# A cross-attention and mixture-of-experts layer: value projections of the second batch moved into the opening, first maxima split by key halves

## Chip, cores and metric

One core of a Trainium2 chip runs the whole layer in one launch. The metric is device time in microseconds (us), from the first to the last instruction of the program with what the launch adds around it; lower is better.

## The reference

Four batches of 512 tokens of width 256. First cross-attention over 1024 context tokens with 16 heads of width 16, rotary positions and a mask; then a second layer with causal self-attention and a mixture of 8 experts, of which each token takes 2.

```python
# x (4,512,256), ctx (4,1024,256), mask (4,1024)
query = split_heads(layernorm(x) @ w_q.T); key = split_heads(ctx @ w_k.T); value = split_heads(ctx @ w_v.T)
query, key = rope(query), rope(key)
scores = einsum('bhqd,bhkd->bhqk', query, key) / sqrt(16)
scores = where(mask == 0, -10000.0, scores)
x = x + (softmax(scores) @ value) @ w_o.T
h = layernorm(x)
h = h + causal_attention(layernorm(h, ln1)) @ proj.T
gate = softmax(layernorm(h, ln2) @ router.T); two best experts of 8
x = x + h + sum_e weight_e * gelu(ln2(h) @ w1_e) @ w2_e
```

The kernel holds every matmul input as a high and a low part, so a projection is three products (high with high, high with low, low with high) over two halves of the width: 6 matmuls of 128x512, or 6 of 128x256 for half a job.

## The kernel before

The change lies in `cross_attention`, the first of three blocks. `attention_order` writes one list of jobs by hand; each engine walks that list and does its own share of every job, in order, waiting on counters of the other engines (`by_pe`, `by_dve`, `by_act`, `by_pool`). The jobs:

- `w`: split of a weight. ACT makes the high part (L575), then DVE or POOL the low part (L467). `wv` and `wo` are POOL's.
- `c(b,g)`: split of half g (512 tokens) of batch b's context, brought by SP into the one buffer `craw`; for b > 0 on POOL (L498, L467).
- `xn`, `xT`, `q`: layer norm, transposition, query projection of a batch.
- `k(b,g,e)` and `v(b,g,n)`: key and value projections of a context half (PE L824). ACT copies each product out (L612) into `turn_a` or `vaug`, except in the first batch's queries and `k(0,0,*)`, which DVE takes.
- `rope(b,part)`: the rotation and its split (function `turn`, L450 to L464), on DVE for `(0,2)` (queries) and `(0,0)`, else on POOL. SP stores its parts to DRAM (`store_turned`), then loads them back in the layout of the scores (`load_queries`, `load_keys`) into `qst` and `kst`, one unit of 8 heads at a time.
- `max(quad,hp,qt,kh)`: 2 score matmuls into one of two `wide` slots (PE L910) and a reduction (DVE L756) that gives row maxima of a quad (4 heads); 16 of these, then `nm` (DVE L760 to L766), `mxt` (PE L915, ACT) and `load_max_rows` on SP bring the maxima into `qst`.
- `rate(1)`: DVE's statistics of batches 1 to 3 (L675 to L686), with a square root on ACT (L566) between.

After the list `before` (the opening) come 128 groups, 32 to a batch. A group is 4 score matmuls (PE L949), 4 exponentials (ACT L618) and 8 weighing matmuls of the group before (PE L964). Between them stand 2 maxima of the next quad, and at most a job or so of projection work for the next batch, placed by the due times in `timed`. Values of batch 1 are projected in half jobs in groups 13 to 20. Projections, scores and `mxt` share three `narrow` PSUM slots in a ring: the job that takes a slot waits until what stood in it three places earlier has been copied out. From group 118 on there are no maxima left and two scores are taken together.

In the opening the order is: `k(0,1,*)`, queries, `k(0,0,*)`, then `wv` and `wo`, the four `v(0,..)`, `rate(1)`, `c(1,0)`, `k(1,0,*)`, `rope(1,0)`, `c(1,1)`, 16 maxima of quad 0, then 4 maxima of quad 1 with the two jobs `k(1,1,*)` among them. POOL's own order follows from it: `rope(0,1)`, `wv`, `wo`, `c(1,0)`, `rope(1,0)`, `c(1,1)`, `rope(1,1)`.

## Time and profile before

| what | value |
|---|---|
| median of 3 runs | 791.83 us (788.49 to 794.24) |
| the profiled execution | 785.16 us, of which the span of instructions is 783.4 us |
| mean granted TensorE clock | 0.948 |

```profile
span 783.4 us, 13504 instructions
## 1 busy us (share of the span) xinstructions
PE 694.3 (89%) x4402; PEld 424.7 (54%) x4402; DVE 557.6 (71%) x919; ACT 493.5 (63%) x980; POOL 354.6 (45%) x262
## 2 busy tenths in 40 slices
PE   2355799999999999999999999879978879999996
PEld 1252344444444443444333433557767768889985
...
ACT  1110567788777788777777778566645057667673
POOL 4867435129440359068658920000055703544444
PEclk9775789999999999999999999999989899999999
DMA  9476257665868473338858820089437456533321
GB/s 264 164 249 184 113 178 245 208 165 192 272 205 238 121 231 114 116 147 282 282 202 291 272 112 2 1 294 421 108 84 251 156 119 139 96 36 36 39 28 20
DMA packets 59719, 130.73 MB, mean 167 GB/s; under 512 B 8868, under 2 KB 26308, under 8 KB 58196
```

Section 1 is busy time; section 2 cuts the span into 40 slices of 19.6 us with a digit of busy tenths each. The opening is the first four to five slices, the groups of the cross-attention run to about the twenty-fifth, and the second layer fills the rest.

### The profile page before, as it was taken

What the parts mean: (1) busy time and instruction counts of PE and PEld (TensorE: products, weight loads), DVE (VectorE), ACT (ScalarE), POOL (GpSimd) and SP (SyncE); (2) the same over time, 40 slices, a digit from 0 to 9 for tenths busy, and PEclk for the clock granted to TensorE, in tenths of its full rate; (3) what the DMA queues carried; (4) which work ended last, traced back from release to release, by engine and by line L of the source; (5) the groups of instructions that cost most, each with busy time, mean ns of one, the idle gap of its engine ahead of it and who ended that gap; (6) DMA issues with size and microseconds to landing.
All of it is one profiled execution on the core that took longest, in us unless ns stands there. A gap on an engine that the chain in (4) does not pass through costs nothing. (4 is left out here: it accounts for less than half of the span.)

```text
span 783.4 us, 13504 instructions
## 1 busy us (share of the span) xinstructions
PE 694.3 (89%) x4402; PEld 424.7 (54%) x4402; DVE 557.6 (71%) x919; ACT 493.5 (63%) x980; POOL 354.6 (45%) x262
## 2 busy tenths in 40 slices
PE   2355799999999999999999999879978879999996
PEld 1252344444444443444333433557767768889985
DVE  4968778778888778887889893367985435555553
ACT  1110567788777788777777778566645057667673
POOL 4867435129440359068658920000055703544444
PEclk9775789999999999999999999999989899999999
DMA  9476257665868473338858820089437456533321
GB/s 264 164 249 184 113 178 245 208 165 192 272 205 238 121 231 114 116 147 282 282 202 291 272 112 2 1 294 421 108 84 251 156 119 139 96 36 36 39 28 20
DMA packets 59719, 130.73 MB, mean 167 GB/s; under 512 B 8868, under 2 KB 26308, under 8 KB 58196
## 3 DMA queue, kind: packets, MB, share of 16 engines
q1 hardware_dynamic: 33364, 72.86, 28.2%
q0 software_dynamic: 16848, 35.95, 17.9%
q10 hardware_dynamic: 9440, 21.06, 9.0%
q8 instruction: 38, 0.62, 0.3%
q14 instruction: 29, 0.24, 0.1%
HBM read 80.80 MB, written 69.39 MB: 192 GB/s over the span
## 5 line engine op out<-in xcount | busy, mean ns | idle before, releaser
L756 DVE TENSOR_REDUCE mx<-wide 128x2 f32<-128x1024 f32 x256 | 307.3, 1222 | 69.3 <-PE wide L910 68.1
L618 ACT ACTIVATE probs<-narrow 128x512 f32<-128x512 f32 x492 | 265.4, 599 | 73.5 <-PE narrow L949 72.3
L910 PE MATMUL wide<-kst,qst 49*128 49x512 f32 x512 | 177.2, 475 | 14.7 <-DMA kst<-k_pieces 7.8
L949 PE MATMUL narrow<-qst,kst 51*128 51x512 f32 x492 | 186.2, 451 | 2.5 <-ACT probs L618 2.2
L949 PEld LDWEIGHTS narrow<-qst,kst 51*128 51x128 f32 x492 | 79.0, 185 | 133.8 <-issue 49.6
L964 PE MATMUL values<-probs,vaug 128*17 128x512 f32 x1024 | 135.3, 600 | 1.4 <-ACT probs L618 0.8
L1714 POOL DMA_INDIRECT out<-res,token x39 | 60.7, 1557 | 94.4 <-DMA out<-res,token 60.5
L910 PEld LDWEIGHTS wide<-kst,qst 49*128 49x128 f32 x512 | 71.4, 194 | 29.4 <-DVE mx L756 16.9
L1246 POOL DMA_DIRECT2D out<-xt x4 | 5.5, 1378 | 113.8 <-DVE xt L1441 113.8
L1739 ACT ACTIVATE h_hi<-narrow 128x512 fp32r<-128x512 f32 x39 | 23.3, 599 | 42.5 <-PE narrow L1819 42.5
L455 POOL TENSOR_TENSOR turn_b<-turn_a,tab 128x1024 f32<-128x1024 f32 x10 | 24.0, 2401 | 55.6 <-ACT turn_a L612 55.1
L1765 DVE TENSOR_TENSOR h_lo<-narrow,h_hi 128x512 fp32r<-128x512 f32 x39 | 27.0, 692 | 23.8 <-ACT h_hi L1739 23.8
L964 PEld LDWEIGHTS values<-probs,vaug 128*17 128x17 f32 x1024 | 17.0, 95 | 44.4 <-issue 29.5
L1253 POOL DMA_INDIRECT list_rows<-lists,rows_to x32 | 32.2, 1008 | 17.2 <-issue 8.5
L1761 DVE TENSOR_TENSOR y_lo<-y_full,y_hi 128x256 fp32r<-128x256 f32 x39 | 16.6, 425 | 30.0 <-ACT y_hi L1726 30.0
L450 POOL TENSOR_SCALAR keep<-keep 128x512 f32<-128x512 int32 x7 | 13.6, 1942 | 51.8 <-ACT turn_a L612 51.8
L1725 ACT ACTIVATE y_full<-wide,lncol 128x128 f32<-128x128 f32 x78 | 35.8, 459 | 0.9 <-PE wide L1796 0.9
L1726 ACT ACTIVATE y_hi<-wide,lncol 128x128 fp32r<-128x128 f32 x78 | 36.3, 465 | 0.0
L498 POOL CAST c_hi<-craw 128x1024 fp32r<-128x1024 f32 x6 | 6.2, 1038 | 59.8 <-PE narrow L824 57.9
L824 PE MATMUL narrow<-wv_hi,c_hi 128*128 128x256 f32 x64 | 16.3, 340 | 15.0 <-POOL wv_lo L467 15.0
L612 ACT ACTIVATE vaug<-narrow 128x256 f32<-128x256 f32 (+1 forms) x28 | 11.6, 416 | 28.3 <-PE narrow L824 27.0
L1810 PE MATMUL wide<-w_hi,y_hi 128*128 x78 | 28.6, 448 | 0.0
(289 smaller groups left out, 1350.3 us busy)
## 6 DMA issues: line engine op xcount, KB each, us to landing
list_rows<-in_w ACTq DMA_DIRECT2D x56, 342.0 KB, 5.4
kst<-k_pieces SPq DMA_DIRECT2D x14, 784.0 KB
k_pieces<-turn_a SPq DMA_DIRECT2D x16, 512.0 KB, 4.3
w_hi<-w_hi SPq DMA_DIRECT2D x16, 512.0 KB, 11.0
w_lo<-w_lo SPq DMA_DIRECT2D x16, 512.0 KB, 11.9
turn_a<-in_w POOLq DMA_DIRECT2D x11, 512.0 KB, 5.3
w_hi<-turn_b POOLq DMA_DIRECT2D x11, 512.0 KB, 3.0
w_lo<-turn_a POOLq DMA_DIRECT2D x11, 512.0 KB, 4.5
```

Source lines behind the costliest of these rows:

```text
L455: step(engine.tensor_tensor(z[:, :, :], a[:, :, :], cos, ALU.mult))
L618: nc.scalar.activation(probs[:, n % NP, :], score_bank(n), ACT.Exp, scale=DK ** -0.5).then_inc(exp_done, 1)
L756: last = nc.vector.tensor_reduce(mx[quad % 2][:, qt, :, hp, kh], slot[:, :, :], axis=AX.X, op=ALU.max)
L910: last = nc.tensor.matmul(slot[:, i, :], qst[u % 3][r:r + R_MAX, h, P * qt:P * qt + P], kst[u % 3][r:r + R_MAX, h, 512 * kh:512 * kh + 512 ...
L949: nc.tensor.matmul(score_bank(n), kst[u % 3][r:r + R_ALL, h, P * kt:P * kt + P], qst[u % 3][r:r + R_ALL, h, :], start=True, stop=True).the ...
L964: last = nc.tensor.matmul(values[32 * hq:32 * hq + DK + 1, :], vaug[b % 2][:, kt, h, :], probs[:, (4 * g + hq) % NP, :], start=kt == 0, st ...
L1253: pool.indirect_dma_start(list_dram, bass.IndirectOffsetOnAxis(rows_to[:, j, i, s:s + 1], 0), lists[j][:, i, s, :].bitcast(U32), None).the ...
L1714: pool.indirect_dma_start(out, bass.IndirectOffsetOnAxis(token[:, n:n + 1], 0), res[n % PIECES][:, :], None, bounds_check=TOKENS - 1, oob_ ...
L1725: nc.scalar.activation(yT[n % 2][:, k, :], y_banks[n % 2][:, k, :], ACT.Identity, **affine)
L1726: last = nc.scalar.activation(yT_hi[n % 2][:, k, :], y_banks[n % 2][:, k, :], ACT.Identity, **affine)
L1765: nc.vector.tensor_tensor(hT_lo[n % 2][:, :, :], h_banks[n % 2], hT_hi[n % 2][:, :, :].bitcast(F32), ALU.subtract).then_inc(h_lo_set, 1)
L1810: last = nc.tensor.matmul(up_banks[n % 2], a[n % 2][:, k, :], w[:, bass.ds(e, 1), k, :].rearrange("p e n -> p (e n)"), start=(i, k) == (0, ...
```

## The change

- `w v` moves ahead of `rope(0,1)` on POOL; `w o` moves behind `c(1,1)`, and on ACT behind `rate(1)`.
- `k(0,0,*)` leaves the ring and is written to the `wide` slots.
- `c(1,1)` gets a landing place of its own (`next_raw`, which is `xn`), loaded early; it moves ahead of `rope(1,0)`.
- A job `heat`: 18 matmuls of the identity that nobody reads, once `rope(0,1)` is done.
- The values of batch 1 (`v(1,..)`, four whole jobs) are projected in the opening, between `k(1,0,*)` and the maxima, and no longer in groups 13 to 20.
- The 16 maxima of quad 0 go by key half: 8 with `kh` = 1, which need only the second half of the keys, then 8 with `kh` = 0. The loads get counters of their own (`quad_in`, `half_in`), and SP loads the first two heads' keys before the other queries.
- `k(1,1,*)` is cut into four half jobs, two straight behind the last maximum and two behind the first two maxima of quad 1. The loads of unit 1 (`load_queries(1)`, `load_keys(1)`) move behind `load_max_rows(0)`.
- The due times of the loop come from a table `PLAN`: group offsets for `xn`/`xT`, `q`, `v`, `c`, `k` and `oP` per batch. Batch 2's queries are now made in batch 0's groups (26 to 30), its keys in groups 9 to 19 (before: 21 to 28); `load_context(2,1)` on SP stands behind the store of batch 1's queries.

The diff without declarations and the lines that only thread the new names through:

```diff
@@ -35,6 +35,10 @@
 
 AHEAD = 4
 LEAD = 3
+PLAN = [(18, (26, 27, 28, 30), (), (3, 12), (9, 10, 11, 14, 16, 17, 18, 19), ()),
+        (None, (), (4, 5, 6, 7, 9, 10, 11, 12), (7, 16), (18, 19, 20, 22, 23, 24, 25, 27), (13, 14, 15, 16)),
+        (-6, (3, 4, 6, 7), (13, 14, 15, 16, 17, 18, 19, 20), (), (), (8, 10, 11, 12)),
+        (None, (), (), (), (), (8, 10, 11, 12))]
 
 
 def final(order, *begin):
@@ -48,24 +52,31 @@
     def maxes(quad):
         return [("max", quad, hp, qt, kh) for hp in range(2) for qt in range(QT) for kh in range(2)] + [("nm", quad), ("mxt", quad)]
 
-    before = [("rate", 0), ("xn", 0), ("w", "q"), ("c", 0, 1), ("w", "k"), ("mask", 0), ("xT", 0), ("k", 0, 1, 0), ("k", 0, 1, 1), ("rope", 0, 1), ("c", 0, 0),
-              ("q", 0, 0), ("q", 0, 1), ("rope", 0, 2), ("k", 0, 0, 0), ("k", 0, 0, 1), ("rope", 0, 0), ("w", "v"), ("w", "o")]
+    before = [("rate", 0), ("xn", 0), ("w", "q"), ("c", 0, 1), ("w", "k"), ("mask", 0), ("xT", 0), ("k", 0, 1, 0), ("w", "v"), ("k", 0, 1, 1), ("rope", 0, 1), ("c", 0, 0),
+              ("q", 0, 0), ("q", 0, 1), ("rope", 0, 2), ("k", 0, 0, 0), ("k", 0, 0, 1), ("rope", 0, 0)]
     before += [("v", 0, g, n) for g in range(2) for n in range(2)]
-    before += [("rate", 1), ("c", 1, 0), ("k", 1, 0, 0), ("k", 1, 0, 1), ("rope", 1, 0), ("c", 1, 1)] + maxes(0)
-    before += [*maxes(1)[:2], ("k", 1, 1, 0), *maxes(1)[2:AHEAD], ("k", 1, 1, 1), ("rope", 1, 1)]
+    before += [("rate", 1), ("c", 1, 0), ("c", 1, 1), ("w", "o"), ("heat", 0), ("k", 1, 0, 0), ("k", 1, 0, 1), ("rope", 1, 0)] + [("v", 1, g, n) for g in range(2) for n in range(2)]
+    before += [("max", 0, hp, qt, kh) for kh in (1, 0) for hp in range(2) for qt in range(QT)] + [("nm", 0)]
+    last = [("k", 1, 1, n // 2, n % 2) for n in range(4)]
+    before += last[:2] + [("mxt", 0)] + maxes(1)[:2] + last[2:] + maxes(1)[2:AHEAD] + [("rope", 1, 1)]
 
     timed = []
     for b in range(B):
         g, t = 32 * b, b + 1
-        if t < B:
-            timed += [(max(g - 6, 0) + n * (1 if b else 0.3), ("xn", t, n)) for n in range(QT)] + [(g + (0.5 if b else 2.5), ("xT", t))]
-            timed += [(g + x, ("q", t, n // 2, n % 2)) for n, x in enumerate((3, 4, 6, 7) if b else (4, 5, 6, 7))] + [(g + 7.5, ("rope", t, 2))]
-            timed += [(g + 13.2 + n, ("v", t, n // 4, n // 2 % 2, n % 2)) for n in range(8)]
-        if t + 1 < B:
-            timed += [(g + 16.5, ("c", t + 1, 0)), (g + 20.5, ("c", t + 1, 1))]
-            timed += [(g + 21.2 + n, ("k", t + 1, n // 4, n // 2 % 2, n % 2)) for n in range(8)] + [(g + 24.5, ("rope", t + 1, 0)), (g + 28.5, ("rope", t + 1, 1))]
+        x, q, v, c, k, o = PLAN[b]
+        if b == 0:
+            timed += [(0.3 * n, ("xn", 1, n)) for n in range(QT)] + [(2.5, ("xT", 1))]
+            timed += [(n + 4.2, ("q", 1, n // 2, n % 2)) for n in range(4)] + [(7.5, ("rope", 1, 2))]
+        if x is not None:
+            r = 2 if b == 0 else t
+            timed += [(g + x + n, ("xn", r, n)) for n in range(QT)] + [(g + x + 6.2, ("xT", r))]
+            timed += [(g + at + 0.2, ("q", r, n // 2, n % 2)) for n, at in enumerate(q)] + [(g + q[-1] + 0.5, ("rope", r, 2))]
+        timed += [(g + at + 0.2, ("v", t, n // 4, n // 2 % 2, n % 2)) for n, at in enumerate(v)]
+        if k:
+            timed += [(g + at + 0.5, ("c", t + 1, n)) for n, at in enumerate(c)]
+            timed += [(g + at + 0.2, ("k", t + 1, n // 4, n // 2 % 2, n % 2)) for n, at in enumerate(k)] + [(g + k[4 * n + 3] + 0.5, ("rope", t + 1, n)) for n in range(2)]
         if b > 0:
-            timed += [(g + 2.2, ("oT", b - 1))] + [(g + x, ("oP", b - 1, n // 2, n % 2)) for n, x in enumerate((8, 10, 11, 12))]
+            timed += [(g + 2.2, ("oT", b - 1))] + [(g + at + 0.2, ("oP", b - 1, n // 2, n % 2)) for n, at in enumerate(o)]
     for quad in range(QUADS - 1):
         timed.append((8 * quad + 9.1, ("out", quad)))
     timed += [(GROUPS - 12.8, ("oT0", B - 1)), (GROUPS - 9.5, ("oP0", B - 1))]
...
 SEAM = {GROUPS: 4, GROUPS + 1: 7, GROUPS + 2: 4, GROUPS + 3: 8}
+HEAT = 18
...
     def in_ring(j):
-        return j[0] in ("q", "k", "v", "mxt", "score", "oP") or j[0] == "out" and j[1] < QUADS - 1
+        return j[0] in ("q", "k", "v", "mxt", "score", "oP") and j[:3] != ("k", 0, 0) or j[0] == "out" and j[1] < QUADS - 1
...
+    c_blocks = [(j[1], j[2]) for j in order if j[0] == "c" and j[1:] not in ((0, 0), (1, 1))]
...
-        def landed(u, heads):
-            return quad_in if u == 0 and heads.start == 0 else stack_in[u % 3]
+        def landed(u, heads, parts=(0, 1)):
+            if u == 0 and heads.start == 0:
+                return half_in if parts == (0,) else quad_in
+            return stack_in[u % 3]
...
@@ -397,6 +412,8 @@
         for b in range(B):
             sp.dma_start(k_dram[b, R_MASK].rearrange("h (k p) -> k h p", p=P),
                          mask_s[KT * b:KT * b + KT, :].unsqueeze(1).to_broadcast([KT, H, P])).then_inc(shut_out[b], 16)
+        sp.wait_ge(*by_pe(("xT", 0)))
+        sp.dma_start(next_raw, io["ctxT"][:, SK + 512:2 * SK].rearrange("(k p) t -> p k t", p=P)).then_inc(next_in, 16)
         sp.wait_ge(ones_in, 12 * 16)
         load_context(1, 0)
         store_turned(0, 2)
@@ -404,39 +421,43 @@
         load_keep(1, 0)
         load_queries(0, slice(0, 2))
         load_keys(0, slice(0, 2), (1,))
-        load_queries(0, slice(2, PAIRS))
         store_turned(0, 0)
         load_keys(0, slice(0, 2), (0,))
+        load_queries(0, slice(2, PAIRS))
         load_keys(0, slice(2, PAIRS))
-        load_context(1, 1)
+        load_keep(1, 1)
+        load_max_rows(0)
         load_queries(1)
         load_keys(1)
-        load_keep(1, 1)
-        load_max_rows(0)
         store_turned(1, 0)
+        load_context(2, 0)
         store_turned(1, 1)
         for b in range(B):
             t = b + 1
             if t + 1 < B:
                 load_keep(t + 1, 0)
                 load_keep(t + 1, 1)
-                load_context(t + 1, 0)
+                if b > 0:
+                    load_context(t + 1, 0)
             load_max_rows(4 * b + 1)
             if t < B:
                 load_keys(2 * t)
                 store_turned(t, 2)
+            if t + 1 < B:
+                load_context(t + 1, 1)
             load_max_rows(4 * b + 2)
             if t < B:
                 load_queries(2 * t)
-            if t + 1 < B:
-                load_context(t + 1, 1)
             load_max_rows(4 * b + 3)
+            if b == 0:
+                store_turned(t + 1, 0)
             if t < B:
                 load_queries(2 * t + 1)
                 load_keys(2 * t + 1)
                 load_max_rows(4 * b + 4)
+            if 0 < b and t + 1 < B:
+                store_turned(t + 1, 0)
             if t + 1 < B:
-                store_turned(t + 1, 0)
                 store_turned(t + 1, 1)
 
     def turn(engine, step, settle, b, part):
...
+                if (b, g) == (1, 1):
+                    pool.wait_ge(next_in, 16)
+                else:
+                    pool.wait_ge(c_in, 16 * (c_blocks.index((b, g)) + 1))
+                raw = next_raw if (b, g) == (1, 1) else craw[:, :, :]
                 pool.wait_ge(*by_pe(last_of("v", b - 1, g)))
-                step(nc.gpsimd.tensor_copy(c_hi[g][:, :, :], craw[:, :, :]))
-                settle()
-                lower(nc.gpsimd, c_lo[j[2]], craw, c_hi[j[2]]).then_inc(pool_done, 1)
+                step(nc.gpsimd.tensor_copy(c_hi[g][:, :, :], raw))
+                settle()
+                nc.gpsimd.tensor_tensor(c_lo[g][:, :, :], raw, c_hi[g][:, :, :].bitcast(F32), ALU.subtract).then_inc(pool_done, 1)
...
+                        act.wait_ge(*by_pool(("c", 1, 1)))
                     act.wait_ge(shift_set, 1)
...
                 pe.wait_ge(*by_splitter(("w", "v")))
+            elif kind == "v" and j[1] == 1 and j[3] == 0:
...
+                last.then_inc(pe_done, 1)
+                return
+            if kind == "heat":
+                pe.wait_ge(*by_pool(("rope", 0, 1)))
+                pe.wait_ge(*by_act(last_of("v", 0)))
+                for i in range(HEAT):
                     last = nc.tensor.matmul(narrow[0][:, 0:P], ident[:, :], ident[:, :], start=True, stop=True)
                 last.then_inc(pe_done, 1)
                 return
...
                 u, h = quad // 2, 2 * (quad % 2) + hp
-                if (quad, hp, qt, kh) == (0, 0, 0, 0):
-                    pe.wait_ge(quad_in, 96)
+                if (quad, hp, qt) == (0, 0, 0):
```

## Rows read from the trace of the kernel before

**Rows 1.** Windows view: busy us and instruction count of each engine, TensorE's granted clock, DMA.

```profile
core 0: us, PE busy (x) PEld busy (x) DVE busy (x) ACT busy (x) POOL busy (x), PEclk, DMA share, GB/s
26.50:41.40 14.90, 0.00 (x0) 0.03 (x1) 14.73 (x9) 0.00 (x0) 14.60 (x8) 0.60 0.38 145
41.40:46.40 5.00, 4.99 (x23) 5.00 (x24) 4.90 (x5) 0.60 (x1) 2.08 (x1) 0.50 0.88 315
46.40:49.70 3.30, 3.26 (x27) 3.06 (x25) 3.30 (x11) 1.20 (x2) 2.68 (x2) 0.97 0.84 199
61.30:79.00 17.70, 12.34 (x32) 4.52 (x32) 16.84 (x15) 0.00 (x0) 11.40 (x7) 0.50 0.65 172
120.00:455.00 335.00, 329.77 (x2160) 146.53 (x2160) 279.38 (x289) 260.27 (x501) 188.81 (x136) 1.00 0.66 211
```

**Rows 2.** Timeline of PE in the opening: start us, us, instructions, idle and releaser.

```profile
25.75 0.61 PE L824 MATMUL narrow<-c_hi,wk_lo 128*128 128x512 f32 x2
...
41.41 0.77 PE L824 MATMUL narrow<-wv_hi,c_hi 128*128 128x256 f32 x2 [15.04 <-POOL wv_lo L467]
...
61.32 1.22 PE L910 MATMUL wide<-kst,qst 49*128 49x512 f32 x4 [7.82 <-DMA kst<-k_pieces]
```

**Rows 3.** Timeline of DVE in the opening.

```profile
29.43 2.71 DVE L462 CAST probs<-probs 128x1024 fp32r<-128x1024 f32 x1
...
32.18 2.17 DVE L464 TENSOR_TENSOR probs<-probs 128x1024 fp32r<-128x1024 f32 x1
...
44.67 0.69 DVE L462 CAST turn_a<-turn_b 128x1024 fp32r<-128x1024 f32 x1
...
45.39 1.23 DVE L464 TENSOR_TENSOR turn_b<-turn_b,turn_a 128x1024 fp32r<-128x1024 f32 x1
...
46.53 4.01 DVE L675 BATCH_NORM_STATS2 stats<-xt 128x6 f32<-128x256 f32 x12
...
62.16 18.19 DVE L756 TENSOR_REDUCE mx<-wide 128x2 f32<-128x1024 f32 x16 [9.75 <-PE wide L910]
```

**Rows 4.** Timeline of ACT: the second square root, a copy, the first exponentials.

```profile
51.73 0.21 ACT L566 ACTIVATE std<-varc 128x12 f32<-128x12 f32 x1 [1.43 <-DVE varc L681]
...
52.19 0.60 ACT L612 ACTIVATE turn_a<-narrow 128x512 f32<-128x512 f32 x1 [0.24 <-PE narrow L824]
...
91.07 2.04 ACT L618 ACTIVATE probs<-narrow 128x512 f32<-128x512 f32 x4
```

**Rows 5.** Timeline of POOL: a weight's low part, a context's split, a query rotation.

```profile
39.02 2.24 POOL L467 TENSOR_TENSOR wv_lo<-probs,wv_hi 128x512 fp32r<-128x512 f32 x1
...
46.94 1.04 POOL L498 CAST c_hi<-craw 128x1024 fp32r<-128x1024 f32 x1 [3.45 <-PE narrow L824]
...
48.06 2.38 POOL L467 TENSOR_TENSOR c_lo<-craw,c_hi 128x1024 fp32r<-128x1024 f32 x1
...
120.24 2.37 POOL L455 TENSOR_TENSOR turn_b<-turn_a,tab 128x1024 f32<-128x1024 f32 x1 [15.07 <-ACT turn_a L612]
...
128.84 2.38 POOL L464 TENSOR_TENSOR turn_b<-turn_b,turn_a 128x1024 fp32r<-128x1024 f32 x1
```

**Rows 6.** Timeline of PE at the seam between opening and loop.

```profile
81.14 1.01 PE L915 MATMUL narrow<-ident,mh 128*8 128x128 f32 x4 [2.20 <-DVE mh L766]
...
88.94 0.50 PE L949 MATMUL narrow<-qst,kst 51*128 51x512 f32 x1
```

**Rows 7.** Timeline of PE in the loop, the weighing matmuls of successive groups.

```profile
141.09 1.05 PE L964 MATMUL values<-probs,vaug 128*17 128x512 f32 x8
...
144.32 1.05 PE L964 MATMUL values<-probs,vaug 128*17 128x512 f32 x8
...
454.93 1.05 PE L964 MATMUL values<-probs,vaug 128*17 128x512 f32 x8
...
457.58 1.05 PE L964 MATMUL values<-probs,vaug 128*17 128x512 f32 x8
```

**Rows 8.** Tile view of craw to 200 us: issue to landing.

```profile
DMA to landing us min/median/max: 4.9/6.5/13.6
```

21 lines of the change are left out of this document (12 added, 9 removed).

## The prediction

> **What bounds the kernel now.** I read the windows view first, stage by stage, then the timelines of the opening, then the waits in the loop. Two different limits show.
>
> In the loop TensorE is the limit: from 120 to 455 us it is busy 329.77 of 335.00 us at a granted clock of 1.00 (2.4 GHz), while VectorE has 279.38 and ScalarE 260.27 [rows 1]. Two weighing matmuls follow each other at 3.23 us in a group with a half projection job (141.09, 144.32) and at 2.65 us in one without (454.93, 457.58) [rows 7]. So a half job taken out of the loop is worth 0.58 us, as long as nothing else takes over.
>
> In the opening nobody is busy throughout; a chain of in-order engines sets the pace. TensorE ends `k(0,0,*)` at 26.4 us and then stands for 15.04 us, because the low part of `wv` comes on GpSimd behind the rotation [rows 2]. It stands 7.82 us more until the first maxima's keys have landed at 61.32 [rows 2]. The 16 reductions then take 18.19 us, 1.14 each, with TensorE at clock 0.50 (1.2 GHz) and 12.34 of 17.70 us busy [rows 1, 3]: VectorE is the limit there, not the clock. The first score comes at 88.94 and the first exponential at 91.07 [rows 4, 6]. What the change is worth is thus (a) how much sooner the maxima start, (b) how much shorter the way from there to the first exponential is, (c) what leaves the loop.
>
> **(a) When the maxima start.** I follow the chain in order.
>
> *`wv` first.* GpSimd's 2.24 us [rows 5] now stand before `rope(0,1)`. The high part is ready somewhat before the rotation's inputs, so I take 1.4 of the 2.24 as delay; the rotation that ended at about 39.0 ends at 40.5 (41.3 if all of it counts). TensorE goes on to `v(0,..)` at once from 26.4: 48 matmuls at 3.26/27 = 0.121 us [rows 1] are 5.8 us, done at 32, not at 49.7. The ring allows it, since `k(0,0,*)` has left it. By itself this gives nothing: the next thing TensorE wants is `c(1,0)`.
>
> *The two contexts.* Each is 1.04 + 2.38, with gaps 3.5 us [rows 5]. GpSimd has `c(1,0)` at 44.0 and `c(1,1)` at 47.5 to 48.2. The heating matmuls (18, bound below by 0.121 and above by twice that, 2.2 to 4.4 us) start at 40.5 and end about when `c(1,0)` does. `k(1,0,*)`, 12 matmuls, and the first of the four `v(1,..)` jobs are done by about 49 to 50.
>
> *The stall that is left.* Then TensorE must wait. `v(1,..)` number two takes the ring slot of `k(1,0,0)`, which ScalarE copies out; and ScalarE walks its list in order, where `rate(1)` and now also `w o` stand ahead of that copy. `rate(1)` needs VectorE's statistics, and these come behind VectorE's rotation of `(0,0)`. Before, that rotation ended at 46.62 (45.39 + 1.23), the statistics began at 46.53 and the root ended at 51.94, 5.3 us after the rotation [rows 3, 4]. Nothing in the change makes the rotation earlier. It may make it later: before, its last steps ran while GpSimd was done, and now GpSimd splits the two contexts beside them. The same step beside a busy GpSimd took 2.71 us (29.43) against 0.69 (44.67) for the cast, and 2.17 (32.18) against 1.23 (45.39) for the difference [rows 3]. So the delay is between 0 and 2.0 + 0.9 = 3.0 us. I take 1.7, since each of VectorE's steps would end just behind a GpSimd step, the last one beside the low part of `c(1,1)` at about 48.2. The rotation ends at 48.3 (46.6 to 49.6), the root at 53.6.
>
> The Trainium skill (SBUF — State Buffer, Who interferes with whom) says that a VectorE instruction with two SBUF inputs, or a cast in a two-port mode, and a GpSimd instruction that reads SBUF shut each other out for a whole instruction, and that one with a single input outside those modes doesn't. By that rule the delay is my 1.7 us, without it the rotation ends at 46.6 and the maxima start 1.7 us sooner.
>
> After the root ScalarE makes `wo`'s high part and copies `k(1,0,0)`, 0.6 us each (the 0.60 of 52.19) [rows 4]: TensorE resumes at 54.8. It has then stood some 5 us. Over the 14.9 us of idleness of before, the mean clock was 0.60, so it had fallen to 1.2 GHz soon, and the dense work after it ran 5.0 us at 0.50 before it rose [rows 1]. Of the 36 matmuls left, 23 go at 4.99/23 = 0.217 us and 13 at 0.121: 6.6 us. The maxima start at 61.4, against 61.32. **Gain 0.** With the early end of the rotation and a high clock it is 46.6 + 5.3 + 1.2 + 36 x 0.121 = 57.5, a gain of 3.8; with the late end and all at 0.217 it is 63.9, a loss of 2.6.
>
> The split by key halves brings nothing here. Before, the keys landed 61.32 - 46.62 = 14.7 us after the rotation that made them [rows 2, 3]. By the same 14.7 the second half's land at 40.5 + 14.7 = 55.2, some 6 us before TensorE is free, and the first half's at 48.3 + 14.7 = 63.0; these are wanted only 8 x 1.14 = 9.1 us after the start, at 70.5. That cover of 7 us is what hides the keys' landing. Without it (b) begins later by as much. What the dense values do is to fill the idle stretch with work from the loop, at no price.
>
> **(b) From the first maxima to the first exponential.** Before: 91.07 - 61.32 = 29.75 us. After, with S the start: the last maximum's matmuls end at about S + 17.9 (80.35, the end of the reductions, less one of 1.14, less 61.32). Two half jobs of `k(1,1,*)` follow at once, 12 x 0.217 = 2.6 us, under the last reduction and `nm`, where TensorE stood 2.20 us [rows 6]. `mxt` (1.01) runs from S + 20.5 to 21.5, four matmuls of two maxima to 22.7, the last two half jobs to between 24.2 and 25.3 by the clock. From the end of the last `k` job to the first exponential I keep the 2.1 us of before (copy and function table; 91.07 - 88.94) [rows 4, 6]: S + 26.3 to 27.4. The maxima's trip through SP runs beside it. Before it took at most 88.94 - 82.15 = 6.8 us [rows 6], which would put the first exponential at S + 28.8 at worst. Gain between 1.0 and 3.4; I take **2.6**. Unit 1's queries and keys are now issued behind these rows, at about S + 24; they are wanted for the maxima of group 5, over 15 us later, so they cost nothing; if they were late, TensorE would stand in group 5.
>
> **(c) The loop.** Eight half jobs of `v(1,..)` leave: 8 x 0.58 = **4.6 us**. The bound above is 48 x 0.121 = 5.8; below I take half, 2.3, in case VectorE, whose two reductions are 2.3 of the 2.65 us, sets the pace where groups without jobs now stand together. The other jobs move (keys of batch 2 to groups 9 to 19, its queries to 26 to 30) at the same number, each worth its 0.58 in either place: 0, with 1 us of either sign for meetings with transpositions.
>
> **Sum.** 0 + 2.6 + 4.6 = 7.2 us. The span goes from 783.4 to 776.2, the profiled execution from 785.16 to 778.0. The runs shown have their median 6.7 us above the profiled one, so as a median 791.83 - 7.2 = 784.6 us, 0.9% less. The second layer doesn't change.
>
> **Rivals.**
> *The opening comes in full.* VectorE's rotation isn't slowed and the clock is kept up by the heating: a gain of 3.8 in (a), 3.4 in (b), 5 in (c), about 12 us: 779.6. For it: no step of GpSimd need fall on VectorE's. Against: a clock of 0.50 after every long stand of before [rows 1].
> *The loop doesn't give it back.* VectorE or a ring slot paces the groups and (c) is 0: 789.2. Against it stand the 2.65 us groups of before [rows 7].
> *Slower: a context comes late in the loop.* `c(2,1)` is now loaded behind the store of `rope(1,2)`, in SP's order. That rotation took from 120.24 to 131.22 [rows 5]; 2.6 us sooner it ends at 128.6, its three stores are issued by 130.7, the load lands 6.5 us later (4.9 to 13.6) [rows 8], the split takes 3.5: 140.7. `k(2,1,..)` stands first in group 16, whose weighing was at 144.32 [rows 7]; 2.6 sooner and with a half job more before it, TensorE gets there at about 144. The slack is 3 us. A landing of 13.6 would stall it by 4 us (788.6). It is a loss from a landing of 6.5 + 3 + 7.2 = 16.7 us on, and over 1% slower from about 25, longer than any shown. A stall of 16 us at that place would give 793 to 800.
>
> **How the numbers follow.** My forecast (781 to 788): 0.52. The opening in full: 0.18. The loop without its gain: 0.18. Slower than before: 0.12, of which 0.10 by over 1%. About 1% is what a measurement of this kernel can tell from no change; it lies at 783.9, just beside my number. Faster by over 1% takes 0.18 and half of the forecast, 0.44; within 1% the rest, 0.46. The range is 777 to 793: it leaves out about one in ten on either side.
>
> **What the changed profile would show.** TensorE without a stand between 26 and 32; a stand of some 5 us ending near 55, released by ScalarE's copy and not by a transfer; the root at 53 to 54; the first maxima near 61; the first exponential near 88.5; weighing matmuls 2.65 us apart in groups 12 and 13; no wait on GpSimd's `c_lo` near 144. The forecast is wrong if ScalarE's copy of `k(1,0,0)` comes near 48, if the clock stays at 1.00 through `v(1,..)`, or if groups without a job stay at 3.2 us.

## The result and the profile after

| | before | changed kernel |
|---|---|---|
| median of 20 runs | 791.9 us | 788.0 us |
| ratio of the runs | | 0.9949, 95% interval 0.9932 to 0.9966 |
| the profiled execution | 785.16 us | 787.19 us |
| its span | 783.4 us | 785.4 us |

The change makes the kernel 0.5% faster, some 4 us, where 7.2 us were forecast. Yet the two profiles shown say that it got 2 us slower. How both can be is part of what follows. Ratios here and below leave out two runs, of 860 and 1060 us, whose granted clock was 0.74 and 0.56 where all others had 0.93 or more. From the page of the changed kernel, its busy time and the slices of the clock:

```profile
span 785.4 us, 13602 instructions
## 1 busy us (share of the span) xinstructions
PE 704.1 (90%) x4450; PEld 435.5 (55%) x4450; DVE 557.7 (71%) x919; ACT 493.2 (63%) x978; POOL 356.1 (45%) x262
...
PEclk9976799999999999999999999999987699999999
```

The chain of the opening is the one that was forecast. The timeline of TensorE (start us, us, instructions, idle before and its releaser):

```profile
30.55 0.40 PE L851 MATMUL narrow<-wv_hi,c_lo 128*128 128x256 f32 x2
37.62 6.44 PE L923 MATMUL narrow<-ident 128*128 128x128 f32 x36 [6.67 <-POOL turn_b L485]
...
55.28 0.80 PE L851 MATMUL narrow<-wv_hi,c_hi 128*128 128x256 f32 x2 [7.06 <-ACT turn_a L639]
```

TensorE runs on through the first values to 31 us, where before it stood for 15 us [rows 2]. It then stands twice: for GpSimd's rotation, which the heating job is written to wait for (the job itself takes 6.44 us, where 2.2 to 4.4 were forecast), and for 7.06 us, released by ScalarE's copy of `turn_a` and by no transfer, as said (55.28, forecast 54.8). The first maxima's matmuls follow at 61.51.

The timeline of VectorE, from the cosine step of its rotation (0,0) to the first reductions:

```profile
35.60 3.04 DVE L476 TENSOR_TENSOR turn_b<-turn_a,tab 128x1024 f32<-128x1024 f32 x1
...
40.65 2.73 DVE L480 TENSOR_TENSOR turn_b<-turn_b,turn_a 128x512 f32<-128x512 f32 x1
43.30 1.52 DVE L481 TENSOR_TENSOR turn_b<-turn_b,turn_a 128x512 f32<-128x512 f32 x1
44.85 2.79 DVE L483 CAST turn_a<-turn_b 128x1024 fp32r<-128x1024 f32 x1
47.68 1.23 DVE L485 TENSOR_TENSOR turn_b<-turn_b,turn_a 128x1024 fp32r<-128x1024 f32 x1
...
62.05 18.20 DVE L783 TENSOR_REDUCE mx<-wide 128x2 f32<-128x1024 f32 x16 [7.35 <-PE wide L946]
```

The steps that took 1.65 to 0.69 us took 2.73, 1.52 and 2.79 us, and the rotation ends at 48.91 [rows 3]. ScalarE's second root and first exponentials, then GpSimd's last step of `c(2,1)`:

```profile
54.02 0.21 ACT L591 ACTIVATE std<-varc 128x12 f32<-128x12 f32 x1 [22.43 <-DVE varc L708]
...
86.97 2.41 ACT L645 ACTIVATE probs<-narrow 128x512 f32<-128x512 f32 x4
```

```profile
139.15 2.38 POOL L525 TENSOR_TENSOR c_lo<-craw,c_hi 128x1024 fp32r<-128x1024 f32 x1
```

The root is at 54.02 (forecast 53.6) and the first exponential at 86.97 (forecast 88.5) [rows 4]. In the loop, the weighing matmuls of groups 11 and 12 and the first half job of `k(2,1)`:

```profile
131.14 1.05 PE L1000 MATMUL values<-probs,vaug 128*17 128x512 f32 x8
...
133.79 1.05 PE L1000 MATMUL values<-probs,vaug 128*17 128x512 f32 x8
...
144.40 0.50 PE L851 MATMUL narrow<-c_hi,wk_hi 128*128 128x256 f32 x2
```

A group without a job still takes 2.65 us [rows 7], and `c(2,1)` was done at 141.53, 2.9 us before TensorE wanted it (forecast: 3 us).

Milestones, one profile each, in us from the span's start. x_before and x_after are the two kernels cut off behind the cross-attention, of which more below; before_again and after_again are second profiles.

| | first reduction | first exponential | fifth weighing | last weighing | from there to the end |
|---|---|---|---|---|---|
| before | 62.16 | 91.07 | 110.22 | 496.98 | 286.4 |
| before_again | 61.77 | 90.52 | 109.88 | 496.34 | 295.8 |
| x_before | 61.27 | 89.17 | 108.11 | 496.53 | |
| after | 62.05 | 86.97 | 107.68 | 489.11 | 296.3 |
| after_again | 64.67 | 89.86 | 110.72 | 491.07 | 295.6 |
| x_after | 62.91 | 87.58 | 109.84 | 491.46 | |

The means of each three: the first reduction comes 1.5 us later with the change (61.7, 63.2), the first exponential 2.1 us sooner (90.3, 88.1), the fifth weighing at the same time (109.4, 109.4), the last weighing 6.1 us sooner (496.6, 490.5). So the opening gave nothing in the end, and the whole gain was made in the loop.

The loop falls into two parts. Up to the 65th weighing the two kernels have different jobs, behind it the same ones. From the fifth to the 65th it took 198.8, 198.7 and 198.8 us before, and 194.1, 194.8 and 194.0 with the change (after, after_again, x_after): 4.4 us less. From the 65th to the last it took 188.0, 187.8 and 189.6 before, and 187.3, 185.5 and 187.7 with it. These 1.6 us between the means are not the change's: they come from waits that differ between profiles of one kernel, as the section on the seam shows.

### The profile page after: what moved, and what is told of

It is laid out like the page before. It is cut to its first block and busy times, and to the rows that moved or that the text cites. A ratio compares the mean times of both kernels' runs of the same rounds, so it can differ in the third digit from the quotient of the medians.

```text
span 785.4 us, 13602 instructions
## 1 busy us (share of the span) xinstructions
PE 704.1 (90%) x4450; PEld 435.5 (55%) x4450; DVE 557.7 (71%) x919; ACT 493.2 (63%) x978; POOL 356.1 (45%) x262
## 3 DMA queue, kind: packets, MB, share of 16 engines
q0 software_dynamic: 16848, 35.95, 17.8%
## 5 line engine op out<-in xcount | busy, mean ns | idle before, releaser
L783 DVE TENSOR_REDUCE mx<-wide 128x2 f32<-128x1024 f32 x256 | 306.7, 1223 | 63.2 <-PE wide L946 62.0
L946 PE MATMUL wide<-kst,qst 49*128 49x512 f32 x512 | 172.6, 466 | 10.4 <-DVE mx L783 9.6
L985 PEld LDWEIGHTS narrow<-qst,kst 51*128 51x128 f32 x492 | 79.2, 186 | 132.6 <-ACT probs L645 54.8
L1606 PE MATMUL narrow<-ident 128*128 128x128 f32 x172 | 26.5, 317 | 9.1 <-issue 5.7
L471 POOL TENSOR_SCALAR keep<-keep 128x512 f32<-128x512 int32 x7 | 13.8, 1968 | 44.9 <-ACT turn_a L639 44.9
L639 ACT ACTIVATE turn_a<-narrow 128x256 f32<-128x256 f32 (+1 forms) x36 | 14.6, 408 | 26.5 <-PE narrow L851 25.2
L1606 PEld LDWEIGHTS narrow<-ident 128*128 128x128 f32 x172 | 24.8, 230 | 9.9 <-issue 8.4
```

Source lines behind the costliest of these rows:

```text
L783: last = nc.vector.tensor_reduce(mx[quad % 2][:, qt, :, hp, kh], slot[:, :, :], axis=AX.X, op=ALU.max)
L946: last = nc.tensor.matmul(slot[:, i, :], qst[u % 3][r:r + R_MAX, h, P * qt:P * qt + P], kst[u % 3][r:r + R_MAX, h, 512 * kh:512 * kh + 512 ...
L985: nc.tensor.matmul(score_bank(n), kst[u % 3][r:r + R_ALL, h, P * kt:P * kt + P], qst[u % 3][r:r + R_ALL, h, :], start=True, stop=True).the ...
L1606: nc.tensor.matmul(bank[:, 0:P], ident[:, :], ident[:, :], start=True, stop=True)
```

## The experiments

Each run of a kernel was set beside runs of the kernel before on the same chip. The three sets ran on three chips, and the medians of before were 792.3, 781.8 and 792.5 us in them, so times are compared as ratios, or within a set.

### Where the gain is: the kernels cut off

```diff
             cross_attention(nc, part, io, xt, wide, narrow, values, ident, mv1, rates, split_dram, list_dram)
+        # write xt to out, wait, return
```

> The kernel before, cut off behind the cross-attention: the second layer and the experts are left out and the state after the cross-attention is written out. It gives, with its partner x_after, the gain of the first block in plain timed runs, not only in one profile. Theory A (the cross-attention gains the whole 7.9 us that the two profiles show at the last weighing matmul, and the second layer gives about 4 of it back): x_after is 7.9 us shorter, 7 to 9. Theory B (the gain in plain runs is smaller than in the profiles, and the second layer isn't changed): x_after is 3 to 5 us shorter. The last weighing matmul of this kernel stands at 497 us in its profile by both.

> The changed kernel cut off in the same way: the second layer and the experts are left out. Theory A: 7 to 9 us below x_before. Theory B: 3 to 5 us below it. The last weighing matmul at 489 us in the profile.

Measured: 515.64 us (514.79 to 517.03) and 511.61 us (508.87 to 512.08), 4 runs each: 4.0 us less. Theory B by its number: in plain runs the cross-attention gains 4 us, and this is all of the whole kernel's gain. By the profiles of the pair it gains 5.1 us at the last weighing; so the first profile's 7.9 us was on the high side of a spread that the table shows. (The comment in the diff stands for the eight lines that do it.)

### The kernel before once more

> The kernel before once more, for a second profile of its second layer, from the last weighing matmul to the end (286.4 us in the first profile; 296.3 in the first profile of the changed kernel). Theory A1 (that stretch varies from run to run, and the first profile was a lucky one: 785.16 us against a median of 791.9): 289 to 295 here, with a stand of TensorE in the heating matmuls of the router's stretch. Theory A2 (the stretch is fixed for each kernel): 286 to 287 again.

Measured: a span of 792.1 us, and 295.8 us from the last weighing to the end, not 286.4. The cross-attention agrees with the first profile within 0.7 us. The first profile of before was the exception, and behind the cross-attention the two kernels take the same time. The waits of TensorE in this profile, from 95 to 145 us behind the last weighing:

```profile
PE narrow L1570 <- issue: 8.0, 9, 1.7
```

In the router's heating matmuls TensorE stood for 8.0 us in 9 pieces with nothing that the profile shows to wait for. In the first profile of before this group has no such row. Six more whole profiles have it: after 5.7 us, rate_late 7.6, no_heat 7.6, after_again 6.8, woven 6.4, woven_whole 6.1. The four of the second set (rate_clear, turn_alone, whole_keys, old_seam) don't; that set's chip is the one on which before took 781.8 us, and this stretch took 283.7 to 287.3 there. It goes with neither kernel, so it has nothing to do with the change.

### The stall behind ScalarE's order

```diff
-    before += [("rate", 1), ("c", 1, 0), ("c", 1, 1), ("w", "o"), ("heat", 0), ..., ("rope", 1, 0)] + [("v", 1, g, n) ...]
+    before += [("c", 1, 0), ("c", 1, 1), ("w", "o"), ("heat", 0), ..., ("rope", 1, 0)] + [("v", 1, g, n) ...] + [("rate", 1)]
```

> The changed kernel with one job moved: rate(1) stands behind the values of batch 1 instead of ahead of c(1,0), so that ScalarE no longer holds the copy of k(1,0,0) back for the second square root. My theory of the stall (ScalarE's order, not the ring, not the clock, not the keys): TensorE's stand of 7.1 us before the second v(1,..) job goes, those jobs end near 52.5 at the high clock, and the first reductions start at the end of VectorE's statistics, near 54.7 against 62.05: the last weighing matmul comes about 7 us sooner (482), and the time is 5 to 7 us below the changed kernel's, 0.985 to 0.988 of before. Rival (the keys' landing or the ring's copies are next in line at once): the first reductions start after 58, and less than 4 us are gained.

Measured: 785.24 us (6 runs), ratio 0.9905 (0.9868 to 0.9942). The stall is gone: the values run through at the high clock and the first maxima's matmuls are issued at 54.01. But the reductions start at 60.15 only. VectorE's timeline in rate_late, two tiny steps of the statistics and the reductions:

```profile
55.99 1.82 DVE L708 TENSOR_SCALAR varc<-mv 128x12 f32<-128x12 f32 x1
...
58.35 1.88 DVE L713 SCALAR_TENSOR_TENSOR shift<-mv,rstd 128x12 f32<-128x12 f32 x1
60.15 18.18 DVE L783 TENSOR_REDUCE mx<-wide 128x2 f32<-128x1024 f32 x16
```

The cause of the stall was right; what follows from it was not. Behind ScalarE stands VectorE itself. Its last rotation step took 2.20 us, beside GpSimd's low part of `wo` and the first step of its rotation (1,0), and two steps on 128x12 elements took 1.82 and 1.88 us (0.17 in the changed kernel), beside later steps of that rotation, which now starts earlier. The rival got the numbers: the first reduction starts after 58 and under 4 us are gained, though for another reason than the keys. The last weighing stood at 489.68 in this profile, where 482 was expected.

```diff
                 pool.wait_ge(tab_in[part % 2], 16)
+                if (b, part) == (1, 0):
+                    pool.wait_ge(shift_set, 1)
```

> rate_late with one wait more: GpSimd starts rope(1,0) only when the statistics' last result (shift) is there. In rate_late the stall of TensorE went, but VectorE's difference took 2.20 us and two tiny steps of the statistics 1.82 and 1.88 (0.17 each before), all beside rope(1,0), and the maxima started at 60.15. Theory (VectorE sets the start of the maxima, and GpSimd's reads hold its steps up): the three steps fall back to 1.23, 0.17 and 0.17, the first reduction comes 4 us sooner than in rate_late, counted from the first transposition, and the time is 3 to 4 us below rate_late's. Rival (the small steps were slow for another reason, or the first groups give it back): no change of the three steps, or a time within 1.5 us of rate_late's.

Measured: ratio 0.9863 (0.9833 to 0.9893), 6 runs. VectorE's timeline in rate_clear:

```profile
54.08 0.17 DVE L710 TENSOR_SCALAR varc<-mv 128x12 f32<-128x12 f32 x1
...
54.79 0.17 DVE L715 SCALAR_TENSOR_TENSOR shift<-mv,rstd 128x12 f32<-128x12 f32 x1
54.88 18.19 DVE L785 TENSOR_REDUCE mx<-wide 128x2 f32<-128x1024 f32 x16
```

The two small steps are back at 0.17, the first reduction stands at 54.88. Counted from the first transposition (13.88 and 12.30) it comes 46.3 and 42.6 us later: 3.7 us gained. The rotation's last step stayed at 2.20, as it still runs beside GpSimd's low part of `wo`. The last weighing is at 481.07. Of the two ratios the difference is 0.4%, some 3 us, with intervals that overlap; the trace settles it.

### GpSimd's splits beside VectorE's rotation

```diff
                 pool.wait_ge(*by_pe(last_of("v", b - 1, g)))
+                if (b, g) == (1, 0):
+                    pool.wait_ge(*by_dve(("rope", 0, 0)))
```

> The changed kernel, but GpSimd splits the two contexts only behind VectorE's rotation (0,0). It measures the contention by itself. If GpSimd's splits hold up the rotation's last steps (2.73, 1.52, 2.79, 1.23 us in the changed kernel; 1.65, 0.68, 0.69, 1.23 before), they fall to about 0.7, 0.7, 0.7, 1.2 here and the rotation ends some 4 us sooner; the root and TensorE's second v(1,..) job move by as much, to the point where the late splits (7 us) and the keys' projection stand in the way. If not, the steps stay as long as in the changed kernel.

Measured in one profile, VectorE's timeline in turn_alone, the cosine step and the last four of the rotation:

```profile
35.45 3.03 DVE L476 TENSOR_TENSOR turn_b<-turn_a,tab 128x1024 f32<-128x1024 f32 x1
...
39.78 0.69 DVE L480 TENSOR_TENSOR turn_b<-turn_b,turn_a 128x512 f32<-128x512 f32 x1
40.39 0.68 DVE L481 TENSOR_TENSOR turn_b<-turn_b,turn_a 128x512 f32<-128x512 f32 x1
41.10 0.69 DVE L483 CAST turn_a<-turn_b 128x1024 fp32r<-128x1024 f32 x1
41.83 1.23 DVE L485 TENSOR_TENSOR turn_b<-turn_b,turn_a 128x1024 fp32r<-128x1024 f32 x1
```

The three steps took 0.69, 0.68 and 0.69 us instead of 2.73, 1.52 and 2.79. The one before them, the sine step, fell from 1.94 to 1.23. From the start of the cosine step to the end of the rotation it is 7.6 us (35.45 to 43.06), 13.3 us in the changed kernel (35.60 to 48.91) and 9.5 us before (37.10 to 46.62). So the change's early splits cost VectorE 3.8 us more than before, and 5.7 us in all. The first reduction came at 57.58, 4.5 us sooner, though GpSimd starts the splits 6 us later.

### The split by key halves

```diff
-    before += [("max", 0, hp, qt, kh) for kh in (1, 0) for hp in range(2) for qt in range(QT)] + [("nm", 0)]
+    before += [("max", 0, hp, qt, kh) for hp in range(2) for qt in range(QT) for kh in (1, 0)] + [("nm", 0)]
```

> The changed kernel with the first maxima in the old nesting (both key halves of a tile, then the next tile), all else the same: it undoes the split by key halves alone. My theory: the keys of both halves have landed before TensorE is through with v(1,..), so the split is worth nothing; the first reduction stays at 62, the first exponential at 87, the time at the changed kernel's, 788 within 1.5 us. Rival (the first half's keys land late): the second maximum waits for a transfer, by up to 3 us, and the time is as much higher.

Measured: ratio 0.9965 (0.9947 to 0.9983), 10 runs, against 0.9949 (0.9932 to 0.9966) and 0.9966 (0.9945 to 0.9986) of the changed kernel in other sets. First reduction 62.95, first exponential 87.69. TensorE's waits up to 100 us in whole_keys:

```profile
PE wide L946 <- DVE mx L783: 7.7, 19, 1.1
PE narrow L851 <- ACT turn_a L639: 7.4, 1, 7.4
```

No wait for `kst` is among them. In the changed kernel the split is worth nothing.

### The seam

```diff
-    last = [("k", 1, 1, n // 2, n % 2) for n in range(4)]
-    before += last[:2] + [("mxt", 0)] + maxes(1)[:2] + last[2:] + maxes(1)[2:AHEAD] + [("rope", 1, 1)]
+    before += [("mxt", 0), *maxes(1)[:2], ("k", 1, 1, 0), *maxes(1)[2:AHEAD], ("k", 1, 1, 1), ("rope", 1, 1)]
```

> The changed kernel with the old order at the seam: mxt straight behind nm, k(1,1,*) as two whole jobs, one behind the second and one behind the fourth maximum of quad 1. In the changed kernel the first exponential came 25.5 us after the first maximum instead of 29.8, but the fourth weighing came only 2.5 us sooner than before, as VectorE then had eight reductions in a row. Theory (the seam's gain is given back to VectorE in the first four groups): the first exponential comes 3 to 4 us later than in the changed kernel, the fifth weighing only 0 to 1.5 us later, and the time is 0 to 1.5 us higher. Rival (the gain at the seam lasts): the fifth weighing and the time are 3 to 4 us later.

Measured: ratio 0.9974 (0.9954 to 0.9995), 10 runs; in the same set whole_keys, which has the new seam, had 0.9965. The first exponential came at 91.11, 28.6 us behind the first reduction (24.9 in the changed kernel, 28.9 before). From there to the fifth weighing it took 19.2 us, in the changed kernel 20.7 to 22.3. Added up, the fifth weighing comes 47.8 us behind the first reduction here and 45.6 to 46.9 in the changed kernel, so of 3.7 us at the first exponential 0.8 to 2.1 are left at the fifth weighing. That is nearer to the theory (0 to 1.5) than to the rival (3 to 4).

Where the rest goes can be read more closely. From the first exponential to the first weighing it took 2.1 us in all three profiles of before and in old_seam (91.07 and 93.17 in before), and 4.4 to 4.5 in those of the changed kernel (86.97 and 91.42). From the first to the fifth weighing the means are alike (17.0 and 16.9). TensorE's timeline in after, between the two:

```profile
86.88 0.50 PE L946 MATMUL wide<-kst,qst 49*128 49x512 f32 x2 [0.43 <-DVE mx L783]
...
88.01 0.49 PE L946 MATMUL wide<-kst,qst 49*128 49x512 f32 x2 [0.39 <-DVE mx L783]
...
90.27 0.79 PE L946 MATMUL wide<-kst,qst 49*128 49x512 f32 x2 [0.40 <-DVE mx L783]
...
91.42 1.91 PE L1000 MATMUL values<-probs,vaug 128*17 128x512 f32 x8
```

Each maximum waits for a reduction, one every 1.13 us (a row like these stands at 89.14 too), and the scores and the first weighing stand behind them. So the gain is given back before the first weighing, by VectorE's row of reductions and not by the clock of the groups behind it.

This profile shows what else moves such numbers. In group 21 of old_seam, VectorE's cast of `mh`, the GpSimd instruction beside it, and TensorE:

```profile
162.29 2.10 DVE L790 CAST mh<-nm 128x16 fp32r<-128x16 f32 x1
```

```profile
162.00 2.37 POOL L472 TENSOR_TENSOR turn_a<-turn_a,keep 128x1024 f32<-128x1024 f32 x1
```

```profile
164.75 0.60 PE L950 MATMUL narrow<-ident,mh 128*8 128x128 f32 x4 [1.32 <-DVE mh L792]
...
166.94 1.91 PE L999 MATMUL values<-probs,vaug 128*17 128x512 f32 x8
```

The cast on 128x16 elements takes 2.10 us and ends with GpSimd's instruction. In the kernel before, in group 93, where GpSimd does nothing, it takes 0.17; in no_heat's group 21 it takes 0.18 beside GpSimd's step before this one (L472 there, TENSOR_SCALAR with one input), so not every GpSimd instruction holds it up. TensorE waits 1.32 us for `mh`, and the weighing behind it takes 1.91 us instead of 1.05: TensorE fell to 1.2 GHz inside the dense loop, and from 165.8 to 172.5 the granted clock is 0.50. Groups 21 to 23 took 12.6 us; in the changed kernel it was 9.4 to 9.6, with waits of 0.65 to 0.87 us there and no fall, and 8.4 in no_heat, without a wait. From the fifth to the last weighing old_seam took 386.1 us, 4.5 to 5.8 more than the changed kernel; 3.0 to 3.2 of it are these groups, the rest shorter waits of the same kind. So its last weighing at 496.37 is mostly not the seam's. I did not expect it, and the median of its runs shows only a part.

The same happens in the kernel before: in x_before the cast takes 2.37 us in group 93, TensorE waits 1.59 us, and groups 93 to 95 take 12.6 us at a clock of 0.73, where every other profile has 8.4. Which groups are hit differs from profile to profile, and so does the outcome: waits of 0.92 and 1.12 us were followed by a fall in woven_whole and woven (group 21), waits of 1.03 and 1.10 in old_seam's groups 101 and 109 were not. The length of the wait alone doesn't decide it.

### The heating job

```diff
+    before.remove(("heat", 0))
```

> The changed kernel without its heating job. My theory: the stand that it bridges is followed by another of 7 us for which ScalarE's order is the cause, so it saves nothing: k(1,0,*) runs at 1.2 GHz and ends later, at about 46 to 48 instead of 46.6, still ahead of the root at 54; the first reduction stays at 62 and the time at the changed kernel's, within 1.5 us. Rival (the clock it keeps up is worth something): the first reduction 2 us later or more, and the time as much higher.

Measured: ratio 0.9936 (0.9911 to 0.9962), 8 runs, beside 0.9966 (0.9945 to 0.9986) of the changed kernel in the same set. Of TensorE's waits up to 100 us in no_heat, the one for ScalarE:

```profile
PE narrow L852 <- ACT turn_a L640: 6.0, 1, 6.0
```

`k(1,0,*)` runs at 1.2 GHz until about 49, the stand for ScalarE shrinks from 7.06 to 6.0 us, and the first reduction is at 64.29 (after_again: 64.67). The heating job is worth nothing where it stands. If anything the kernel is faster without it; the two intervals overlap.

### The changed kernel once more

> The changed kernel once more, beside the others on the same chip, to set their times against. The last weighing matmul stood at 489.1 us in its first profile and at 491.5 and 491.7 in the kernels that are alike up to there (x_after, whole_keys), with TensorE's mean clock in the first four groups at 0.84, 0.67 and 0.66. Theory (what the change gives at the seam goes back in the first groups, by VectorE's row of reductions and by the clock, which falls to a different part of them each time): the last weighing at 489 to 492, the more the higher that clock; ratio 0.993 to 0.997 as before. Rival: a last weighing at 489 with a clock below 0.7.

Measured: ratio 0.9966, last weighing 491.07 with a clock of 0.82 in the first four groups. The windows view from the first to the fifth weighing, of after, x_after and no_heat (the second column is the length, the one behind the busy times the clock):

```profile
91.42:107.68 16.26, 14.51 (x82) 5.91 (x81) 11.81 (x11) 9.80 (x18) 10.02 (x7) 0.84 0.79 292
```

```profile
92.03:109.84 17.81, 16.55 (x81) 7.11 (x80) 11.81 (x11) 9.69 (x18) 11.34 (x8) 0.67 0.78 286
```

```profile
93.88:109.28 15.40, 13.72 (x82) 5.57 (x81) 11.93 (x12) 9.92 (x19) 10.00 (x7) 0.92 0.76 282
```

The same four groups take 15.4 us at a mean clock of 0.92, 16.3 at 0.84 and 17.8 at 0.67; turn_alone had 18.6 at 0.59. Before it was 16.8 to 17.3 at 0.80 or 0.81. So the clock spreads these groups by 3 us. It does not settle where the last weighing falls: after_again has 491.07 at 0.82, after 489.11 at 0.84, because its opening came 2.6 us later. The theory's second half falls with that; of its first half VectorE's row of reductions holds.

### The opening put together

```diff
-    before += [("rate", 1), ("c", 1, 0), ("c", 1, 1), ("w", "o"), ("heat", 0), ("k", 1, 0, 0), ("k", 1, 0, 1), ("rope", 1, 0)] + [("v", 1, g, n) ...]
-    before += [("max", 0, hp, qt, kh) for kh in (1, 0) for hp in range(2) for qt in range(QT)] + [("nm", 0)]
+    before += [("c", 1, 0), ("c", 1, 1), ("w", "o"), ("heat", 0), ("k", 1, 0, 0), ("rate", 1), ("k", 1, 0, 1), ("rope", 1, 0)]
+    halves = [("v", 1, g, n, i) for g in range(2) for n in range(2) for i in range(2)]
+    for m, j in enumerate([("max", 0, hp, qt, kh) for kh in (1, 0) for hp in range(2) for qt in range(QT)]):
+        before += [j] + (halves[m // 2:m // 2 + 1] if m % 2 else [])
+    before += [("nm", 0)]
...
                 pool.wait_ge(*by_pe(last_of("v", b - 1, g)))
+                if (b, g) == (1, 0):
+                    pool.wait_ge(*by_dve(("rope", 0, 0)))
+                if (b, g) == (1, 1):
+                    pool.wait_ge(shift_set, 1)
```

> What the runs so far say of the opening, put together: GpSimd splits the contexts of batch 1 only behind VectorE's rotation (0,0) and its second one only behind the statistics; rate(1) stands between the two key projections, so that ScalarE holds up nothing; the eight half jobs of v(1,..) stand between the 16 maxima, one behind every second. Theory (VectorE's own work is the chain of the opening, from its rotation over the statistics to the 16 reductions): rotation ends at 43 to 44 as in turn_alone, the statistics at 49, the first reduction starts near 50 to 51 instead of 62, still 1.14 us each, and the last weighing matmul stands 9 to 12 us sooner than in the changed kernel; ratio to before 0.980 to 0.984. Rival (TensorE, at 1.2 GHz, can't carry the values between the maxima, or the first half's keys land too late): the reductions come more than 1.3 us apart, and less than 6 us are gained.

Measured: 780.11 us, ratio 0.9836 (0.9807 to 0.9865), 6 runs: 12 us below before and 9.6 below the changed kernel in the same set. VectorE's timeline in woven, the first six reductions and the step behind the last:

```profile
53.40 6.88 DVE L790 TENSOR_REDUCE mx<-wide 128x2 f32<-128x1024 f32 x6 [0.69 <-PE wide L953]
...
74.52 0.19 DVE L794 TENSOR_REDUCE nm<-mx 128x16 f32<-128x32 f32 x1
```

The rotation ends at 44.9 and the first reduction starts at 53.40, 2.5 us later than expected, for two reasons that end within 0.2 us of each other. The root on ScalarE waits for the copy of `k(1,0,0)`, behind a projection that runs at 1.2 GHz, so the statistics end at 52.7; and TensorE comes to the first maxima only at 52.86, since `k(1,0,*)` starts at 48.60, behind GpSimd's later split of `c(1,0)`. The 16 reductions take 21.1 us with the values between them, not 18.2. So part of the rival is true as well: they are 1.32 us apart. The last weighing is at 486.04, 5 us sooner than in after_again; expected were 9 to 12. At the fifth weighing (100.74) it was still 10.0 us sooner. The loop took 385.3 us instead of 380.4 to 381.6, since this profile has a fall of the clock in group 21 too: a wait of 1.12 us for `mh`, and groups 21 to 23 at 12.1 us with a clock of 0.72. It beats both kernels, and rate_clear with 0.9863 does so too.

```diff
-    for m, j in enumerate([("max", 0, hp, qt, kh) for kh in (1, 0) for hp in range(2) for qt in range(QT)]):
+    for m, j in enumerate([("max", 0, hp, qt, kh) for hp in range(2) for qt in range(QT) for kh in (1, 0)]):
```

> woven with the first maxima in the old nesting (both key halves of a tile). In whole_keys the split by key halves was worth nothing, since TensorE came to the maxima long after the keys. Theory (it is worth something only when the maxima can start early): the second maximum waits for the first half's keys, which land some 14 us behind the rotation, near 57 to 58; the last reduction ends 5 to 7 us later than in woven, and the time is 4 to 7 us higher. Rival (the keys are no limit here either): the same as woven within 1.5 us.

Measured: 788.88 us, ratio 0.9953 (0.9923 to 0.9982), 10 runs, 8.8 us above woven, more than the 4 to 7 expected; the step behind the last reduction is at 83.52, 9.0 us later. TensorE's longest waits for one tile up to 100 us in woven_whole:

```profile
PE wide L953 <- DMA kst<-k_pieces: 7.8, 1, 7.8
```

The second maximum stands 7.8 us for the first half's keys. The same edit that was worth nothing in the changed kernel is worth 9 us where the maxima can start early.

## Why the prediction was right, and where its terms were off

The forecast was 784.6 us with a range of 777 to 793. Measured were 788.0, in the range and within 1% of before. The direction held; the gain was about half of the 7.2 us.

- **(a) When the maxima start.** Every step of the chain was there: the first values at once behind `k(0,0,*)`, the stand of TensorE released by ScalarE's copy (55.28 for 54.8), the root (54.02 for 53.6), the values' first part at 1.2 GHz. That the times fit so well in this profile is in part luck: its cosine step started at 35.60, while in the other two profiles of the changed kernel it was 37.71 and 36.90, with the root at 56.11 and 55.31. "Gain 0" was 1.5 us too good by the means (61.7 to 63.2). The mis-sized term is the rotation's delay: I took 1.7 us on its end, bounded by 3.0 from two steps. From the cosine step to its end it was 3.8 us longer in each of the three profiles (13.3 for 9.5), and by the means the rotation ends 4.3 us later (50.0 for 45.8). GpSimd's side was mis-sized as well: its two splits took 9.6 us beside VectorE (37.51 to 47.10), where 7.0 were forecast and 6.9 were measured in turn_alone. I had not counted the first of the last four steps, which was slow before too, and grew from 1.65 to 2.73.
- **The Trainium skill's rule** (SBUF — State Buffer, Who interferes with whom), that a VectorE instruction with two SBUF inputs or in a two-port mode and a GpSimd instruction that reads SBUF shut each other out for a whole instruction, agrees with turn_alone (0.69 us for each of the three steps without GpSimd's splits), and with the statistics, which have one input each and took 4.01 us beside GpSimd and without. The small step on 12 elements that reads two inputs (1.88 for 0.17 us in rate_late) agrees too; the one that reads a single input (1.82 for 0.17 us) does only if it ran in a two-port mode, which the profile does not show.
- **The keys and the heating.** That the split by halves brings nothing was right, and so was it to count nothing for the heating job; whole_keys and no_heat show it.
- **(b) The seam.** The step that failed is the end point. I took the gain at the first exponential, 2.6 us, as gained for good. There it was larger, 3.6 us from the first reduction on (28.5 to 24.9, the means of each three). But from the first exponential to the fifth weighing it took 2.1 us longer (19.2 to 21.3), all of it ahead of the first weighing (2.1 to 4.4). With the two half jobs of `k(1,1,*)` no longer between the maxima, VectorE had eight reductions in a row (9.2 us), and the scores of the first group stand behind maxima in TensorE's order. What is left of (b) is about 1.5 us, and (a) takes it. The four groups' clock, 0.67 to 0.84, adds a spread of 1.5 us.
- **(c) The loop.** In the groups whose jobs differ, 4.4 us were gained, where 4.6 were forecast: this term was right. It is the net of two things that no run takes apart, the eight half jobs that left and the moves of batch 2's jobs. The moves shift single groups by up to 1 us both ways (between before and after, groups 9 and 41 take 1.0 us more, groups 29 and 49 take 1.0 us less), and group 21 gives some 1 us back to the wait for `mh`. From the fifth to the last weighing the profiles show 6.1 us less (386.8, 386.5 and 388.4 us before; 381.4, 381.6 and 380.4 with the change). The rest of that, 1.6 us, lies in groups with the same jobs: 4.2 us are x_before's fall of the clock in groups 93 to 95, and groups 101 and 109 are each up to 1.3 us longer in some profiles of either kernel than in others, by waits ahead of `mxt`.
- **The sum.** By the means of three profiles it is 6.1 us at the last weighing, of which 4.4 belong to the change; in plain runs it is 4.0 us (the cut kernels) and 3.9 us (the whole ones). So (a) lost 1.5 us where nothing was forecast, (b) kept 1.5 of 2.6, and (c) gave 4.4 of 4.6. That there is a gain at all is owed to (c); the opening as a whole was forecast at 2.6 us and gave nothing.
- **The base of the sum.** I took the profile of before as typical but for 6.7 us of launch-to-launch difference. In fact it was also 9.4 us shorter behind the last weighing than its repetition (286.4 and 295.8), 8.0 of them TensorE's stands in the router's heating matmuls, which it lacks. That is why the profile of the changed kernel looked slower.

## What to carry to other kernels

When an engine is taken off a wait, look in its own order and then in the orders of those it waits for: here a square root that nobody needed soon held a copy, behind it stood VectorE's own chain, and behind that GpSimd's reads. A gain at a seam is one only if it is still there some groups later; read the milestone behind the seam, not at it. Where two kernels have the same work over a stretch, a difference there is the measure of chance: take it off before the rest is called a gain. And an edit that is worth nothing (loads by halves) can be worth 9 us once the bound ahead of it has gone, so it should be tried again after each such step.

## What the runs showed of the hardware that was not expected

- A VectorE step on 128x12 elements that takes 0.17 us alone took 1.82 to 2.19 us beside GpSimd's instructions (rate_late, turn_alone); a cast on 128x16 elements took 2.10 and 2.37 us for 0.17 (old_seam, x_before).
- One wait of 1.32 us inside a loop that keeps TensorE busy was followed by some 6.7 us at 1.2 GHz and cost 3 us (old_seam, groups 21 to 23). It was so after waits of 1.12 and 1.59 us too (woven, x_before), but not after 1.03 and 1.10 us (old_seam, groups 101 and 109).
- TensorE stood 5.7 to 8.0 us in pieces of up to 2.4 us among matmuls that wait for nothing the profile shows, in seven whole profiles of twelve; it did not in the first profile of before, nor in the four of the set on the chip on which the kernel before took 781.8 us and not 792. What causes it was not tried.
